# Scores of an attention stage regrouped into 36 full banks a pass, with a third score bank and a half-sized accumulator

## The reference, cut to what matters

```
qkv = jnp.einsum('bhce,ef->bhcf', xh, Wqkv) + bqkv        # 8 sequences of 1024 tokens, 16 heads of 16
q, k, v = jnp.split(qkv, 3, axis=-1)
att = jnp.einsum('bhqe,bhke->bhqk', q, k) / jnp.sqrt(jnp.float32(he))
mask = jnp.tril(jnp.ones((c, c), dtype=att.dtype), k=-1)
att = jax.nn.softmax(att * mask, axis=-1)
out = jnp.einsum('bhqk,bhke->bhqe', att, v)
out = out @ Wr + br
```

## Time and profile before

| | us |
|---|---|
| median of three runs | 3116.52 (3113.19 to 3118.41) |
| the profiled execution's own time | 3119.1 |
| its span, first to last instruction | 3117.4 |
| TensorE busy in the span | 2667.5 (86%) |
| VectorE busy | 2095.9 (67%) |
| GpSimd busy | 1723.0 (55%) |
| ScalarE busy | 1582.6 (51%) |
| mean granted TensorE clock | 0.917 of full speed |

### The profile page before, as it was taken

The page is one execution under the profiler, slowest core; times in us unless marked ns, Lnnn a source line. Parts: engine busy times, 40 slices in busy tenths (PEclk is TensorE's granted clock), DMA queues, the critical chain, the costliest instruction groups (busy, mean ns, idle before and its releaser), DMA issues. The chain is left out here.

```text
span 3117.4 us, 61062 instructions
## 1 busy us (share of the span) xinstructions
PE 2667.5 (86%) x15254; PEld 1524.7 (49%) x15318; DVE 2095.9 (67%) x5668; ACT 1582.6 (51%) x3630; POOL 1723.0 (55%) x3076
## 2 busy tenths in 40 slices
PE   1788888888888888888886898898989979999999
PEld 0233333333333333333335666666666646666666
DVE  2656666666566666666637899898989976555554
ACT  1345555555555555555540555555555534444444
POOL 3664344334443344443434787776777747677776
PEclk7779989889889899898996999999999979999999
DMA  3343332442323433334312000000000000000000
GB/s 54 92 106 58 52 56 46 61 65 47 57 49 52 68 52 57 52 50 61 62 51 88 1 1 1 1 1 1 1 1 1 1 1 14 15 15 15 15 15 19
DMA packets 81303, 113.30 MB, mean 36 GB/s; under 512 B 25100, under 2 KB 37144, under 8 KB 80536
## 3 DMA queue, kind: packets, MB, share of 16 engines
q1 hardware_dynamic: 76360, 101.44, 19.1%
q0 software_dynamic: 3072, 8.39, 0.9%
q10 hardware_dynamic: 1744, 2.16, 0.2%
HBM read 18.98 MB, written 8.39 MB: 9 GB/s over the span
## 5 line engine op out<-in xcount | busy, mean ns | idle before, releaser
L509 ACT ACTIVATE probs<-scoresT 128x512 f32<-128x512 f32 (+3 forms) x1536 | 691.4, 490 | 613.9 <-PE scoresT L653 599.5
L600 DVE TENSOR_REDUCE cand<-ring 128x4 f32<-128x512 f32 x1152 | 719.2, 681 | 330.8 <-PE ring L703 272.0
L653 PE MATMUL scoresT<-stage 98*128 98x512 bf16 (+3 forms) x1536 | 493.5, 367 | 100.0 <-ACT probs L509 87.5
L429 POOL TENSOR_SCALAR_AFFINE_SELECT probs<-probs 128x128 f32<-128x128 f32 x1024 | 292.8, 296 | 487.4 <-ACT probs L509 482.2
L667 PE MATMUL pv<-probs,Vg 128*32 128x512 f32 (+3 forms) x3072 | 313.8, 513 | 45.9 <-POOL probs L429 45.9
L653 PEld LDWEIGHTS scoresT<-stage 98*128 98x128 bf16 x1536 | 128.2, 99 | 391.9 <-ACT probs L509 275.0
L703 PE MATMUL ring<-Km,Qm 64*128 64x512 bf16 (+2 forms) x1792 | 250.2, 322 | 70.0 <-DMA Km<-parts 28.3
L1130 PE MATMUL mm<-w_W,hT 128*128 128x256 f32 x1024 | 257.3, 397 | 8.4 <-ACT z L1218 3.4
L1150 PE MATMUL mm<-w_W,x2T 128*128 128x512 f32 x512 | 244.4, 600 | 0.3 <-DVE x L1369 0.2
L1211 ACT ACTIVATE hT<-mmT,w_be,w_g 128x128 f32<-128x128 f32 x512 | 185.5, 469 | 89.1 <-PE mmT L1141 89.1
L703 PEld LDWEIGHTS ring<-Km,Qm 64*128 64x128 bf16 x1792 | 82.4, 95 | 302.5 <-issue 115.8
(11 more groups left out here) (254 smaller groups left out, 5293.1 us busy)
## 6 DMA issues: line engine op xcount, KB each, us to landing
stage<-parts SPq DMA_DIRECT2D x256, 96.0 KB, 2.8
stage<-parts SPq DMA_DIRECT2D x256, 64.0 KB, 2.8
Qm<-parts SPq DMA_DIRECT2D x128, 128.0 KB, 2.6
Km<-parts SPq DMA_DIRECT2D x128, 128.0 KB, 2.7
stage<-parts SPq DMA_DIRECT2D x256, 32.0 KB, 2.4
out<-result SPq DMA_DIRECT2D x64, 128.0 KB, 1.7
stage<-ct SPq DMA_DIRECT2D x128, 4.0 KB
w_W<-in_W SPq DMA_DIRECT2D x4, 512.0 KB
```

Source lines behind the costliest of these rows:

```text
L429: nc.gpsimd.affine_select(out=d, in_=d, compare_op=ALU.is_gt, fill=0.0, base=0, pattern=[[1, P]], channel_multiplier=-1).then_inc(mask_ok, 1)
L509: nc.scalar.activation(probs[:, n % 8, lo:hi], scoresT[u % SCORE_BANKS][:, lo % 512:(hi - 1) % 512 + 1], ACT.Exp, scale=SOFT).then_inc(exp ...
L600: ins = nc.vector.tensor_reduce(c, src[:].rearrange("p (t a b) -> p t a b", t=c.shape[1], b=P), AX.X, ALU.max)
L653: nc.tensor.matmul(scoresT[u % SCORE_BANKS][:, lo % 512:(hi - 1) % 512 + 1], Ks[0:ROWS, gi, hh, P * kt:P * kt + P], Qs[0:ROWS, gi, hh, lo: ...
```

## The change

- **Scores.** A pass now has 36 slots of exactly 512 columns instead of 48 units. A slot is one or two matmuls into one bank, then one exponential of 512 columns. kt 1 shares a slot with kt 3, two heads of kt 2 share one, in the upper half kt 5 with kt 7 and two heads of kt 6. All queries below 512 come first (slots 0 to 9), then those from 512 (slots 10 to 35).
- **Banks.** Three score banks instead of two; `pv` has one bank of 512 columns instead of two, which is first used for the queries below 512, copied (`PV_COPY` half 0, position 14), and used again for those from 512.
- **PV bursts.** Six instead of eight, each over two key tiles: at positions 9 and 12 for the lower half, 20 and 28 for the upper, and kt 4/5 and 6/7 at positions 0 and 3 of the next pass.
- **Masks.** 16 instructions of two 128-column blocks each instead of 32 of one.
- **probs** has 16 buffers of 512 columns instead of 8 of 1024.
- **Positions.** 36 of them; the table `AT` is new. For gi 0, MX starts at 2 (was 4), XT at 7 (6), V at 21 (14), VG at 5 (0), OT at 24 (21). PT is split: its first half no longer waits for the second half's bursts.

Matmuls, their columns, the max products and all DMAs are the same in number and size.

```diff
-SCORE_BANKS, RING_BANKS = 2, 4
+SCORE_BANKS, RING_BANKS = 3, 4
+PROBS = 16
...
+    a0 = [[(0, hh, 0, 512)] for hh in range(HPG)]
+    a1 = [[(1, hh, P, 512), (3, hh, 3 * P, 512)] for hh in range(HPG)]
+    slots = a0[0:2] + a1[0:2] + a0[2:4] + a1[2:4]
+    slots += [[(2, hh, 2 * P, 512), (2, hh + 1, 2 * P, 512)] for hh in (0, 2)]
+    slots += [[(kt, hh, 512, S)] for kt in range(5) for hh in range(HPG)]
+    slots += [[(5, hh, 5 * P, S), (7, hh, 7 * P, S)] for hh in range(HPG)]
+    slots += [[(6, hh, 6 * P, S), (6, hh + 1, 6 * P, S)] for hh in (0, 2)]
...
+BURSTS = [(0, (0, 1)), (0, (2, 3)), (1, (0, 1)), (1, (2, 3)), (1, (4, 5)), (1, (6, 7))]
+BURST_AT = {0: 9, 1: 12, 2: 20, 3: 28}
...
-        at(pos_of["PV_LAST"], ("PV", -1, 7))
-        at(pos_of["PV_COPY"], ("PV_COPY", -1))
+        at(0, ("PV", -1, 4))
+        at(3 if scores else 0, ("PV", -1, 5))
+        at(pos_of["PV_COPY"], ("PV_COPY", -1, 1))
...
-        pv = ctx.enter_context(nc.psum_tensor("pv", [P, S], F32))
+        pv = ctx.enter_context(nc.psum_tensor("pv", [P, 512], F32))
...
+                                nc.gpsimd.affine_select(out=d, in_=d, compare_op=ALU.is_gt, fill=0.0, base=0,
+                                                        pattern=[[0, 2], [1, P]], channel_multiplier=-1).then_inc(mask_ok, 1)
...
+                            wait(act, pv_ok, len(BURSTS) * G + bursts_for(slot))
+                            act.wait_ge(st_ok, UNITS * G + slot + 1)
+                            nc.scalar.activation(probs[:, buffer(slot), :], scoresT[slot % SCORE_BANKS][:],
+                                                 ACT.Exp, scale=SOFT).then_inc(exp_ok, 1)
...
+                            elif b == 2:
+                                pe.wait_ge(pvS_ok, 2 * v + 1)
+                            pe.wait_ge(mask_ok, len(MASKS) * v + masks_for(b))
+                            pe.wait_ge(exp_ok, UNITS * v + exps_for(b))
```

More of the change, by code:

```diff
@@ L52, with score_slots @@
 FUTURE = -2.0 ** 126
-SCORE_BANKS, RING_BANKS = 2, 4
[L57 to L71, removed]
+SCORE_BANKS, RING_BANKS = 3, 4
+PROBS = 16
+def score_slots():
+    a0 = [[(0, hh, 0, 512)] for hh in range(HPG)]
[5 more added lines that the diff above has]
+    slots += [[(6, hh, 6 * P, S), (6, hh + 1, 6 * P, S)] for hh in (0, 2)]
+    return slots
@@ new lines, with buffer @@
+SLOTS = score_slots()
+UNITS = len(SLOTS)
+assert UNITS % SCORE_BANKS == 0 and all(sum(hi - lo for _, _, lo, hi in runs) == 512 for runs in SLOTS)
+def buffer(slot):
+    return slot % PROBS if slot < 2 * PROBS else slot - 2 * PROBS + HPG
+RUNS = {}
+for slot_, runs_ in enumerate(SLOTS):
+    column_ = 0
+    for kt_, hh_, lo_, hi_ in runs_:
+        RUNS[kt_, hh_, lo_ // 512] = (slot_, column_, lo_ % 512)
+        column_ += hi_ - lo_
+BURSTS = [(0, (0, 1)), (0, (2, 3)), (1, (0, 1)), (1, (2, 3)), (1, (4, 5)), (1, (6, 7))]
@@ new lines, with masks_for, exps_for @@
+BURST_AT = {0: 9, 1: 12, 2: 20, 3: 28}
+MASKS = ([(1, None), (2, 384), (3, 384), (5, None), (6, 384), (7, 384), (8, 256), (9, 256), (27, None), (29, None)]
+         + [(slot, 384) for slot in range(30, 34)] + [(34, 256), (35, 256)])
+def masks_for(burst):
+    last = max(RUNS[kt, hh, BURSTS[burst][0]][0] for kt in BURSTS[burst][1] for hh in range(HPG))
+    return sum(slot - (second is None) <= last for slot, second in MASKS)
+def exps_for(burst):
+    return 1 + max(RUNS[kt, hh, BURSTS[burst][0]][0] for kt in BURSTS[burst][1] for hh in range(HPG))
@@ L74, with bursts_for @@
+def bursts_for(slot):
+    before = [x for x in range(slot) if buffer(x) == buffer(slot)]
+    back = 0 if before else len(BURSTS)
+    user = before[-1] if before else max(x for x in range(UNITS) if buffer(x) == buffer(slot))
+    last = max(b for b, (half, kts) in enumerate(BURSTS) for kt in kts for hh in range(HPG) if RUNS[kt, hh, half][0] == user)
+    return last + 1 - back
 STAGE = 2 * HPG * S
-UNITS = TPB * HPG + TPB // 2 * HPG
-assert UNITS % SCORE_BANKS == 0
 def wait_apart(eng, *waits):
@@ L149, in window @@
             at(int(lo + (hi - lo) * (n / len(uses)) ** pos_of["MX_CURVE"]), *u)
-        at(31, ("R", "CT", "dve", PAIRS_MX - 1))
+        at(UNITS - 1, ("R", "CT", "dve", PAIRS_MX - 1))
     if scores:
         at(pos_of["EQ"], ("EQ",))
+        at(pos_of["PV_HALF"], ("PV_COPY", 0, 0))
     events = []
-    for pos in range(32 if scores else max(others, default=-1) + 1):
+    for pos in range(UNITS if scores else max(others, default=-1) + 1):
         if scores:
[L156 to L159, removed]
+            events.append(("S", pos))
+            events += [("PV", 0, b) for b, last in BURST_AT.items() if last == pos]
         events += others.pop(pos, [])
@@ L651, in run @@
-                            for u, lo, hi in score_units(kt, hh):
-                                wait(pe, exp_ok, UNITS * G + u + 1 - SCORE_BANKS)
-                                nc.tensor.matmul(scoresT[u % SCORE_BANKS][:, lo % 512:(hi - 1) % 512 + 1],
-                                                 Ks[0:ROWS, gi, hh, P * kt:P * kt + P],
-                                                 Qs[0:ROWS, gi, hh, lo:hi], start=True, stop=True).then_inc(st_ok, 1)
+                            if slot in (0, HPG):
+                                pe.wait_ge(shift_in[slot // HPG], 16 * 2 * (G + 1))
@@ new lines, in run @@
+                            wait(pe, exp_ok, UNITS * G + slot + 1 - SCORE_BANKS)
+                            at = 0
+                            for kt, hh, lo, hi in SLOTS[slot]:
+                                ins = nc.tensor.matmul(scoresT[slot % SCORE_BANKS][:, at:at + hi - lo],
+                                                       Ks[0:ROWS, gi, hh, P * kt:P * kt + P],
+                                                       Qs[0:ROWS, gi, hh, lo:hi], start=True, stop=True)
+                                at += hi - lo
```

79 lines of the change are left out of this document (36 added, 43 removed).

## The result

| median, us | before | after |
|---|---|---|
| four runs each, same chip | 3116.63 | 3004.89 |
| the profiled execution's own time | 3119.1 | 3005.22 |
| its span | 3117.4 | 3002.8 |
| mean granted clock | 0.917 | 0.928 |

The ratio is 0.9643, 95% interval 0.9626 to 0.966: 112 us faster. The forecast was 3042 us (2955 to 3125).

A forecast was written before the change was run, and what follows sets the result against it. TensorE, busy 86% of the span, was taken as the bound. Gains of 1.8 + 0.5 + 1.6 + 0.7 + 0 = 4.6 us a half batch, times 16, made 74 us: 3119.1 − 74 − 2.6 = 3042 us, range 2955 to 3125.

The forecast's parts named there:

- A third score bank: Scores on TensorE wait for the exponential three slots back instead of two: 1.8 us gained a half batch, bounds 0 and 2.4.
- the halved masks: On GpSimd, 16 masks a pass instead of 32 relieve an engine that waits anyway; counted as nothing.
- The bound of 2.4: Most that 0.49 us more slack each could remove from nine score waits outside the turns, 2.4 us a half batch.
- Fewer exponentials: On ScalarE, 12 fewer instructions save 0.8 us a pass, covered by TensorE's other work, so nothing on the path.
- The turn gi 0 to gi 1: TensorE's holes there, before scores and PV, shrink from 1.9 to 1.4 us: gain 0.5 a half batch, bounds 0.2 and 1.0.
- The turn gi 1 to gi 0: Stretch from the last max product to the ring read gets shorter: gain 1.6 us a half batch, bounds 1.0 and 3.4.
- Clock: TensorE's half-clock time: 0.7 us gained at the turn to gi 0, 0 at the other turn, per half batch.
- Signs: Expected profile marks: 1152 exponentials of one form, half batch near 91 us, stated waits, low clock 5 to 10 us.
- The clock did not stay high: Rival: TensorE's clock stays high at both turns, 152 us gained, 2965 us; chance 20%.
- It did not stay low longer either: Rival: five score slots paced by exponentials, then a hole, keep gi 1 longer at half clock, 3126 us; chance 15%.
- The waits move to VectorE's ring reads: Rival: ring reads set the pace and waits move there from the exponential, no change, 3110 to 3123 us; chance 8%.

The follow-up runs named there:

- single_masks: The changed kernel with 32 masks of one block a pass instead of 16 of two: 3026.51 us, ratio 0.9721.
- the square: The changed kernel's order with 48 units or 36 full slots, each with two or three score banks: 3143.8, 3006.7, 3010.5 and 3004.9 us.

## Why the prediction was right, and where it was not

**The direction and the mechanism.** Right: scores wait less for the exponential, TensorE stays the bound, and no other engine takes its place. The gain is 112 us, against 74.

**A third score bank, 1.8 us a half batch.** This is the mis-sized term. The half batch gained 6.9 us (95.63 to 88.74); the turns gave 0.9 of it and the clock at most 2.1 (both below), so 3.9 to 6.0 are left for this term and for the halved masks, whose part is 1.1 (`single_masks`). In the ledger, which counts turns and clock in, the scores gave 11.1. I priced the waits by the idle column of the scores' row, 5.2 us. Time that the profile calls busy more than doubled that: 28.5 us of "busy" scores for the same columns that now take 22.0. That exposed weight loads and gaps inside folded rows make it up is my reading; low clock is a part of it too. The bound of 2.4 was no bound, since it stood on the same column. The attribution was also wrong: the bank alone is worth 137 us with narrow units and 6 with full ones (the square, clock counted in). Full banks, which I counted as fewer exponentials at zero, do the same work as the bank.

**Fewer exponentials, zero.** Right as ScalarE time: doubling them costs 5 us at most. Wrong as a statement on full banks, as above. That a narrow unit holds its bank for longer than its share of columns (0.27 us of exponential for 128 columns, 0.60 for 512, and the same two hand-overs) fits the square, but I measured no hand-over by itself.

**The turn gi 0 to gi 1, 0.5 us.** Right. PV waits until 431.25, 3.8 us after the last max product's end (forecast 3.9); the holes of the turn are 0.25 + 0.45 + 0.77 = 1.5 us against 1.9. The two-block mask is 0.41 us alone and 1.84 / 5 = 0.37 in a queue (estimate 0.4). But the halved masks, a term that I put at nothing, are not free: singles cost 21.6 us.

**The turn gi 1 to gi 0, 1.6 us.** Too good. PV starts 3.8 us behind the last max product (forecast 3.9), and from there to the ring read's end the walk was right in order: root behind the mask of slot 3, `xn` behind it. Its sizes were not. From 375.50 to 392.00 it takes 16.5 us, where I had 13.6 to 16.0, and the gain by the same working is 16.0 + 0.95 − 16.5 = 0.45 us, below my lower bound of 1.0. The walk took `xn` at 2.14 us and met 3.87. I had noted the running sums beside it and looked only at GpSimd's own lateness. The hole of 2 to 3 us was 5.96.

**Clock, 0.7 and 0.** Low clock fell by 3.4 us in the half batch shown, 17.0 to 13.6, and by 4.3 in the mean of the twelve. With TensorE at work in all of it that is at most 1.7 and 2.1 us, so 0.7 can be of the right size; the forecast of 5 to 10 us of low clock was too good. The low stretch at the other turn kept its 3.4 us.

**Signs.** 1152 exponentials of one form: right. gi 0 near 51 us: 51.5. gi 1 near 40: it was 37.7, and the half batch 89 instead of 91. Wait on the exponential 1 to 2 us: 1.1. Mask wait at PV of kt 4/5, 1 to 2 us: it was less, 0.77 and 0.29. Wait at the third max pair, 2 to 3 us: right in place, but 5.96. No new wait of over 1 us at the bursts at 9, 12 and 20: right in the loop, wrong in the last half batch, where the burst at position 9 waits for a mask that stands behind the running sums of V. I had named those sums and trusted the ring reads to cover them; there they do not:

```profile
1456.76 2.01 PE L717 MATMUL pv<-probs,Vg 128*32 128x512 f32 x16 [2.26 <-POOL probs L476]
```

**The rivals.** The clock did not stay high. It did not stay low longer either. By the Trainium skill ("TensorE: Matmul & The Clock Gate", "A second HAM failure mode: psum-queue depth-cycling") the runs of full slots could have brought the clock down again and again; here low clock shrank in sum, though it comes in three stretches a half batch instead of two, and was longer with three banks (166.6) than with two (133.1). It grew to 251.6 us in the long window in the 48-unit kernel with two banks, the one with the most waits. "The waits move to VectorE's ring reads" was half true: waits at max products grew by 6.5 us, of which 3.0 came from PT. The bank's term, with the masks, was 2.1 to 4.2 us too small and the second turn's 1.15 us too large, so the sum came out nearer than its parts; that part is luck.

## What to carry to other kernels

The idle column of a matmul row was far below what its waits cost here. Look at the waits of its weight loads, and take start-to-start times, before you price slack on a PSUM bank; the waits of the weight loads are no price by themselves (74 us fewer of them with the third bank, and 6 us less time). Fuller banks and more banks bought the same slack: take one, and price the second at what is left, best with the 2 by 2 square. After a gain, look at what stands ahead of the now latest chain on an in-order engine: moving one small GpSimd step ahead of a mask was worth 42 us, more than a third of the change itself.

## What the runs showed of the hardware

VectorE's `xn` (one SBUF input of 128x128 f32) takes 340 ns by itself, in the mean 401 to 453 where GpSimd's masks or `tmp` run beside it, and 550 beside GpSimd's additions of two SBUF inputs; in the half batch shown, up to 620:

```profile
L620 DVE TENSOR_SCALAR xn<-h,mv,rstd x8: 335/610/620, 387.5 to 391.0; 128x128 f32 x8
```
```profile
L501 POOL TENSOR_TENSOR Rsum<-Rsum,Vh x6: 452/452/453, 387.9 to 390.6; 128x128 f32<-128x128 f32 x6
```

GpSimd's additions take 452 ns there and 455 where `xn` is elsewhere, so only VectorE pays. The Trainium skill ("SBUF — State Buffer", "Who interferes with whom") describes a pair of ports that VectorE and GpSimd share under an exclusive lock, for which a VectorE `tensor_scalar` in a two-port mode competes; the added 0.28 us at most (340 to 620 here) are less than one whole addition, and that only VectorE paid is this trace's own.

One exponential of 512 columns cut into two of 256 in ScalarE's queue costs 0.058 us more. A mask of two 128-column blocks costs 0.37 us in a queue, of one block 0.26.
